# Products of ones in the gaps of `l1_attn`, a rolling order in `l1_slots`, one joined stage for `l1_combine` and `l2_attn`, and a new order in `l3_xattn`

## The reference

```python
# L1_attn: a self attention with running states; per head of 8 features, d = 8
#   states after each token = cumulative sum of outer products of k and a gradient of a layer norm,
#   applied to k (first pass) and to q (second pass), then a group norm and an output product
# L1_ffn: 64 experts, 6 per token, capacity 64, and one shared expert
scores = softmax(xf @ gate_w.T); idx = top_k(scores + gate_b, 6)
xb = zeros((64, 64, D)).at[se, pos].set(xf[tok], mode='drop')
h = silu(einsum('ecd,eid->eci', xb, w1)) * einsum('ecd,eid->eci', xb, w3)
yb = einsum('eci,edi->ecd', h, w2)
y = zeros_like(xf).at[tok].add(contrib * wf[:, None])
z = silu(xf @ ws1.T) * (xf @ ws3.T) @ ws2.T          # x + (y + z)
# L2_attn: linear attention
q, k, v = split(layernorm(x) @ W_qkv.T, 3); q = relu(q) + 1e-6; k = relu(k) + 1e-6
kv = einsum('bnd,bne->bde', k, v); z = 1 / (einsum('bnd,bd->bn', q, k.sum(1)) + 1e-6)
x + einsum('bnd,bde,bn->bne', q, kv, z) @ W_out.T + b_out
# L3_xattn: 16 heads of 8 features, 128 queries against 120 context rows, softmax, output product
```

## Time and profile before

| What | us |
|---|---|
| Median of 3 runs | 4386.08 |
| Lowest and highest run | 4382.82 and 4388.71 |
| The profiled execution, device time | 4399.44 |
| Its span, first to last instruction | 4397.5 |
| Mean granted clock | 0.817 |
| TensorE busy (share of the span) | 3267.4 (74%) |
| VectorE busy | 2842.7 (65%) |
| ScalarE busy | 1802.4 (41%) |
| GpSimd busy | 681.8 (16%) |

### The profile page before, as it was taken

One profiled execution on the slowest core, in us unless ns is written; L12 is line 12 of the kernel. 1 busy time (PEld: TensorE's weight loads), 2 busy tenths in 40 slices (PEclk: granted clock), 3 DMA queues, 4 the chain that ended last, 5 costly groups with the idle time before them and its releaser, 6 DMA issues. The chain is left out here.

```text
span 4397.5 us, 70729 instructions
## 1 busy us (share of the span) xinstructions
PE 3267.4 (74%) x22305; PEld 2394.5 (54%) x22369; DVE 2842.7 (65%) x8231; ACT 1802.4 (41%) x5188; POOL 681.8 (16%) x867
## 2 busy tenths in 40 slices
PE   3668379366654886755777876999899997786887
PEld 3546269222222664534454754666577775554777
DVE  6556633499995876174898263555467775556997
ACT  1346334111112664212777233222155553435886
POOL 0045533100002777200000120000100000000000
PEclk9789589666666665577788685999999998998999
DMA  4040168200004000420300011333200000000000
GB/s 116 1 166 0 33 195 234 73 0 0 0 0 154 3 0 1 126 95 18 74 0 0 1 38 34 103 100 99 86 1 0 0 0 4 0 0 15 1 0 19
DMA packets 135723, 196.88 MB, mean 45 GB/s; under 512 B 24858, under 2 KB 90840, under 8 KB 133846
## 3 DMA queue, kind: packets, MB, share of 16 engines
q1 hardware_dynamic: 124078, 186.31, 14.0%
q0 software_dynamic: 11520, 9.05, 0.7%
HBM read 151.49 MB, written 58.63 MB: 48 GB/s over the span
## 5 line engine op out<-in xcount | busy, mean ns | idle before, releaser
L1260 PE MATMUL l_attn_p_s<-l_attn_outer,l_attn_upper 128*128 128x512 f32 x256 | 204.5, 973 | 113.9 <-DVE l_attn_outer L1203 100.0
L95 POOL TENSOR_TENSOR rstd<-vareps,minus_half 128x32 f32<-128x32 f32 x11 | 59.9, 5444 | 1391.7 <-DVE vareps L86 1258.0
L2583 ACT ACTIVATE l_ffn_sg<-l_ffn_p_g 128x512 f32<-128x512 f32 x168 | 100.3, 597 | 355.4 <-PE l_ffn_p_g L2620 355.4
L2554 DVE TENSOR_TENSOR l_ffn_part<-l_ffn_sg,l_ffn_share 128x512 f32<-128x512 f32 x168 | 116.3, 693 | 190.8 <-ACT l_ffn_sg L2583 183.3
L2610 PEld LDWEIGHTS l_ffn_p_o<-l_ffn_wd,l_ffn_h 128*128 128x128 f32 x1344 | 175.7, 191 | 85.2 <-issue 76.1
L1418 POOL DMA_INDIRECT slots_in<-l_xattn_x,l_xattn_slot x192 | 190.3, 991 | 83.8 <-issue 49.9
L1260 PEld LDWEIGHTS l_attn_p_s<-l_attn_outer,l_attn_upper 128*128 128x128 f32 x256 | 79.2, 324 | 218.7 <-issue 174.4
L2730 ACT ACTIVATE l_attn_E<-l_attn_p_s,l_attn_nm 128x128 f32<-128x128 f32 x512 | 181.2, 386 | 2.9 <-DVE l_attn_nm L2688 2.9
L2610 PE MATMUL l_ffn_p_o<-l_ffn_wd,l_ffn_h 128*128 128x128 f32 x1344 | 178.1, 275 | 2.3 <-DVE l_ffn_h L2557 1.6
L2620 PE MATMUL l_ffn_p_g<-l_ffn_f_xTall,l_ffn_wg 128*128 (+1 forms) x336 | 173.7, 599 | 0.5 <-DVE l_ffn_turned L2545 0.5
L2622 PE MATMUL l_ffn_p_u<-l_ffn_f_xTall,l_ffn_wu 128*128 (+1 forms) x336 | 172.5, 595 | 0.0
(11 more groups left out here) (806 smaller groups left out, 9436.5 us busy)
## 6 DMA issues: line engine op xcount, KB each, us to landing
l_experts_w<-in_L_ffn_w SPq DMA_DIRECT2D x72, 512.0 KB
l_ffn_share<-share_rows SPq DMA_DIRECT2D x112, 256.0 KB, 3.2
slots_in<-l_xattn_empty SPq DMA_DIRECT2D x8, 2145.0 KB, 24.0
shares_out<-l_xattn_zero SPq DMA_DIRECT2D x24, 512.0 KB, 11.5
l_combine_got<-shares_out SPq DMA_DIRECT2D x16, 768.0 KB, 4.5
l_attn_toep<-kernel_rows SPq DMA_DIRECT2D x1, 8192.0 KB, 31.1
xattn_toep<-ssm_rows SPq DMA_DIRECT2D x1, 8192.0 KB
l_slots_w<-in_L_ffn_w SPq DMA_DIRECT2D x32, 176.0 KB
```

What stands on the lines that cost most here:

```text
L1260: mm = pe.matmul(p_s[:, r, a], upper[:], outer[:, r, a * 512:(a + 1) * 512], start=True, stop=True)
L2554: dve.tensor_tensor(part[:, w], sg[:, w], share[:, slot], ALU.mult).then_inc(s.share_used, 1)
L2583: act.activation(sg[:, k], p_g[:, k], ACT.Silu).then_inc(s.silu_ready, 1)
```

## The change

Four stages change, and one short fill is added.

1. `kept_warm` multiplies a bfloat16 tile of ones by itself, 128 x 512 per product, and nobody reads the result. In `l1_attn` TensorE makes ten of them ahead of the second running state, four ahead of the transposes of the context, and four ahead of the means of squares. They go into `p_t` and `p_c`, which are overwritten later by the transposes.
2. `l1_slots`: all programs are written out in steps (transposes at lag 0, hidden products at lag 1, down products at lag 2), and inputs have four buffers instead of two.
3. `l1_combine` and `l2_attn` become one stage `l1_out` of 16 pairs and lags 0 to 4, written out. Three of the six results are added on GpSimd and three on TensorE, as products with the identity into the bank of the down product. The norm is made per pair, with the power of two columns on GpSimd and the normalisation on ScalarE; the bias is added on GpSimd.
4. `l3_xattn`: L2952 and L2956 move behind L2961, and the output product goes to columns 256 to 384 of `p_c` instead of `p_r`; on VectorE the copy of the keys comes ahead of the addition to `x`, and the statistics come last.

The diff, cut to its core:

```diff
+def kept_warm(R, pe, bank, n):
+    for _ in range(n):
+        pe.matmul(bank, R.onesb[:], R.onesb[:].unsqueeze(1).broadcast_to((P, 4, P)), start=True, stop=True)
 # l1_attn, tensor
                     for b, u in item(2):
+                        for c, _ in item(1):
+                            pe.wait_ge(s.xT_ready, c + 1)
+                        kept_warm(R, pe, p_t[:], 10)
...
                     for b, u in item(3):
+                        kept_warm(R, pe, p_c[:], 4)
                         pe.wait_ge(s.ctx_ready, b + 1)
...
                     for b, u in item(2):
+                        for c, _ in item(0):
+                            kept_warm(R, pe, p_t[:], 4)
                         pe.wait_ge(s.squares_ready, b + 1)
 # l1_slots, tensor
-                with pe.Fori(0, NP // W) as i:
-                    for u in range(W):
-                        pe.wait_ge(x_in[u], (i + 1) * DMA)
-                        pe.transpose(p_x[:, u, 0:P], x[:, u, 0:D], R.ident[:]).then_inc(s.xT_psum, 1)
...
+                for item in written_out(2, NP, V):
+                    for n, u in item(0):
+                        pe.wait_ge(x_in[u], (n // V + 1) * DMA)
+                        after(pe, s.xT_ready, n - 1)
+                        pe.transpose(p_x[:, n % 2, 0:P], x[:, u, 0:D], R.ident[:]).then_inc(s.xT_psum, 1)
+                    for n, u in item(1):
+                        pe.wait_ge(s.xT_ready, n + 1)
+                        pe.wait_ge(up_in[u], (n // V + 1) * DMA)
+                        after(pe, s.h_ready, n - 1)
...
+                    for n, u in item(2):
+                        pe.wait_ge(s.h_ready, n + 1)
 # l1_out, sync
+                for tile, name in ((wg, "L1_ffn_ws1"), (wu, "L1_ffn_ws3"), (wd, "L1_ffn_ws2")):
+                    sp.dma_start(tile[:], A[name][0:1].rearrange("a p n -> p (a n)")).then_inc(s.w_in, DMA)
+                load(sp, A, s.w_in, [(wqkv, "L2_attn_W_qkv"), (wout, "L2_attn_W_out"), (bout, "L2_attn_b_out")])
 # l1_out, tensor
+                pe.wait_ge(s.w_in, 6 * DMA)
+                for item in written_out(4, PAIRS):
...
+                    for b, u in item(1):
+                        after(pe, s.x_added, b)
+                        pe.wait_ge(got_in[u], (b // V + 1) * DMA)
+                        for n in range(SPLIT, K):
+                            pe.matmul(p_d[:, 0:W], R.ident[:], got[:, u, :, n], start=(n == SPLIT), stop=False, skip_group_check=True)
+                        pe.wait_ge(s.h_ready, b + 1)
+                        for r in range(2):
+                            for f in range(FC):
+                                mm = pe.matmul(p_d[:, r * P:(r + 1) * P], h[:, u % 2, f, r * P:(r + 1) * P], wd[:, f * P:(f + 1) * P],
+                                               start=False, stop=(f == FC - 1), skip_group_check=True)
+                        mm.then_inc(s.down_psum, 1)
...
 # l1_out, gpsimd
+                    for b, u in item(2):
+                        pool.wait_ge(s.xhat_ready, b + 1)
+                        pool.tensor_tensor(pair(R.x, b), pair(R.x, b), both(bout), ALU.add).then_inc(s.xb_ready, 1)
+                    for b, u in item(0):
+                        pool.wait_ge(got_in[u], (b // V + 1) * DMA)
+                        for n in range(SPLIT):
+                            add = pool.tensor_tensor(pair(R.x, b), pair(R.x, b), got[:, u, :, n], ALU.add)
...
+                    for b, u in item(1):
+                        pool.wait_ge(s.var_ready, b + 1)
+                        pool.tensor_tensor(rs[:, u % 2], ve[:, u % 2], R.minus_half[:, 0:2], ALU.pow).then_inc(s.rstd_ready, 1)
 # l3_xattn, tensor
-                    for b, u in item(4):
-                        pe.matmul(p_r[:, 0], headsT[:], wo[:], start=True, stop=True).then_inc(s.out_psum, 1)
                     for b, u in item(2):
                         pe.wait_ge(s.shift_spread, b + 1)
-                    for b, u in item(1):
-                        pe.matmul(p_c[:, 0:SC], wkv[:, 0:P], cT[:, u % 2], start=True, stop=True).then_inc(s.kT_psum, 1)
-                    for b, u in item(2):
...
                         mm.then_inc(s.shifted_psum, 1)
+                    for b, u in item(4):
+                        pe.matmul(p_c[:, 256:384], headsT[:], wo[:], start=True, stop=True).then_inc(s.out_psum, 1)
+                    for b, u in item(1):
+                        pe.matmul(p_c[:, 0:SC], wkv[:, 0:P], cT[:, u % 2], start=True, stop=True).then_inc(s.kT_psum, 1)
                     for b, u in item(3):
                         pe.wait_ge(s.oT_ready, b + 1)
-                        after(pe, s.out_taken, b)
+                        after(pe, s.heads_ready, b)
```

More of the change, by code:

```diff
@@ L1788, in _ @@
             def _(sp):
-                with sp.Fori(0, NP // W) as i:
-                    for u in range(W):
[L1791 to L1800, removed]
+                for n in range(NP):
+                    after(sp, s.xT_psum, n + 1 - V)
+                    after(sp, s.meta_ready, n + 1 - V)
+                    sp.dma_start(x[:, n % V], xs[n]).then_inc(x_in[n % V], DMA)
+                    after(sp, s.hid_psum, n + 1 - V)
+                    sp.dma_start(w13[:, n % V], A["L1_ffn_w13"][n]).then_inc(up_in[n % V], DMA)
+                    after(sp, s.y_psum, n + 1 - V)
+                    sp.dma_start(w2[:, n % V], A["L1_ffn_w2"][n]).then_inc(down_in[n % V], DMA)
             @block.gpsimd
@@ L1813, in _ @@
             def _(act):
[L1814 to L1825, removed]
-                        after(act, R.stored[(n - 1) % V], (n - 1) // V * DMA)
-                        act.activation(y[:, (n - 1) % V], p_y[:, u, 0:P], ACT.Copy, scale=part[:, (n - 1) % V]).then_inc(s.y_ready, 1)
+                for item in written_out(2, NP, V):
+                    for n, u in item(1):
+                        act.wait_ge(s.hid_psum, n + 1)
+                        act.activation(sg[:, n % 2], p_h[0:FP, n % 2, 0:P], ACT.Silu).then_inc(s.silu_ready, 1)
+                    for n, u in item(0):
+                        act.wait_ge(s.xT_psum, n + 1)
+                        after(act, s.hid_psum, n - 1)
+                        act.activation(xT[:, n % 2], p_x[:, n % 2, 0:P], ACT.Copy).then_inc(s.xT_ready, 1)
+                    for n, u in item(2):
+                        act.wait_ge(s.y_psum, n + 1)
+                        act.wait_ge(s.meta_ready, n + 1)
+                        after(act, R.stored[u], n // V * DMA)
+                        act.activation(y[:, u], p_y[:, n % 2, 0:P], ACT.Copy, scale=part[:, u]).then_inc(s.y_ready, 1)
@@ L2035 @@
-PHASES.append(l2_attn)
 LAYOUTS.append(lambda a: {"L2_attn_W_qkv": transposed(a, "L2_attn_W_qkv"), "L2_attn_W_out": transposed(a, "L2_attn_W_out"),
@@ L2885, in _ @@
                                           ALU.mult).then_inc(s.heads_ready, 1)
+                    for b, u in item(4):
+                        if isinstance(b, int):
+                            dve.wait_ge(s.out_taken, b + 1)
+                        chain(dve.bn_stats(R.bn[:, u], row(R.x, b)))
+                        chain(dve.bn_aggr(R.aggr[:, u], R.bn[:, u]))
+                        if u == PER - 1:
+                            dve.tensor_copy(R.stats[:, bass.ds(b - (PER - 1), PER), :], R.aggr[:, 0:PER])
             @block.scalar
@@ L3232, in decoder @@
         R.ones = sb("ones", [P, P])
+        R.onesb = sb("onesb", [P, P], BF16)
         R.ctxT = sb("ctxT", [DC + 1, NB, SC])
```

342 lines of the change are left out of this document (171 added, 171 removed).

## The result

The changed kernel takes **4256.89 us** (median of 4 runs, 4253.62 to 4261.88) against 4387.4 us for the kernel before on the same chip (4 runs): a ratio of 0.9704, 95% interval 0.9687 to 0.9721, or 130.5 us less. Predicted were 4268 us, 118 us less, in a range of 4236 to 4312. The profiled execution took 4255.3 us (span 4253.5), against 4399.4 us of the one before.

A forecast was written before the change was run, and what follows sets the result against it. Bounds were read per stretch: VectorE in `l1_attn`, TensorE in `l1_slots` and `l3_xattn`, engines taking turns in `l1_combine` and `l2_attn`. Terms -17 - 4 - 78 - 19 = -118 us gave 4268 us on the median, range 4236 to 4312.

The forecast's parts named there:

- Ones, -17: In `l1_attn`, products of ones make the first running state fast in most periods: 80% of VectorE's 20.7 us of waits go.
- the lower price: In `l1_attn`, a 512-column product of ones costs 0.41 us at half clock, half a float32 record; the upper bound was 0.88.
- a fast second state lengthens the gap ahead of the context to some 5 us: In `l1_attn`, a second state at full clock ends 3 us earlier; the following 2.3 us gap grows, four products filling 0.9.
- clock above 0.85: Sign to look for afterwards: the clock of `l1_attn` is above 0.85; it averaged 0.66 before.
- Rival (b): In `l1_attn`, the ones don't hold the clock for the first state; 17 us go, giving 4285 us; chance 17%.
- Slots, -4: In `l1_slots`, the new order hides TensorE's idle 4.5 us of 77.5; -4 us, from -8 to +5.
- Rival (c): `l1_slots` reaches full clock once its gaps are closed: 32 us more gained, 4236 us; chance 7%.
- Joined stage, -78: `l1_combine` and `l2_attn` joined: TensorE bounds steps of 7.8 us, the stage takes 142 us against 219.8.
- Rival (a): The joined stage goes by its chain, not by TensorE: 10 us a step gives 4296 us, 11 gives 4309; chance 17%.
- `l3_xattn`, -19: In layer 3's cross attention, two products moved beside the exponential save 0.63 us in about 30 periods; between -12 and -20.
- L2952 and L2956 stand in it from 3810.04 to 3810.67, 0.63 us: In `l3_xattn`, these two products lie in the period's chain of scores, maximum, transposed scores, shift and exponential, costing 0.63 us.
- Rival (d), late instructions: Written-out steps on TensorE and SP wait for instructions, 4.5 us each: +243 us, 4511 us; chance 2%.

The follow-up runs named there:

- ones_ten: Changed kernel keeping only the ten products of ones ahead of the second running state, both groups of four removed: 4266.4 us in one execution, `l1_attn` 536.3 us.
- out_chain: Changed kernel with two more unread powers of two columns on GpSimd ahead of the real one in each `l1_out` step: steps 7.44 us, stage 10.6 us longer.
- slots_first: Changed kernel with two bfloat16 products of ones behind each pair's transpose in `l1_slots`, for the first 8 of 32 pairs only: stage 78.7 us, against 82.3.
- x3_switch: Changed kernel with one 16-column bfloat16 product between the two groups of 32-row products in `l3_xattn`: stage 282.9 us (+10.3), one execution.

## Why the prediction was right

The time lies in the range, and in each of the four stages the wait or idle time that was named is what went. Two sizes were off to the good side by some 9 and 6 us, and `l1_attn` fell 2 us short; one step of the working for `l1_attn` did not happen.

- **Ones, -17, measured -14.7.** The waits fell to 5.1 us as forecast, and a product of ones took 0.23 us at full clock and 0.445 at half (4.45 us for ten), so the lower price was the right one, and at full clock half of it. The Trainium skill ("TensorE: Matmul & The Clock Gate", Back-to-back issue gap) has 0.43 at half clock; the measured 0.445 agrees. Missing was the wait behind: the output product gave 2.3 us back. The remark that a fast second state lengthens the gap ahead of the context to some 5 us is right for `ones_ten` (5.06), but it is not what the changed kernel does. The ten were priced at half clock, where they fill two thirds of the gap; at full clock they fill 2.3 of 6.5 us, and the second state takes 5.1 to 6.6 us in every period. The first state takes 3.70 us in about half of the periods and some 5.3 in the others, and VectorE waits for a state only four times in all. So the size of the gain came out though the second state never was fast, which is luck in that step. The sign "clock above 0.85" was narrowly missed (0.84) and is a poor one: 0.74 came with no gain at all. Rival (b) is what `ones_ten` shows, and not what the change does.
- **Slots, -4, measured -4.6.** TensorE was busy for 66.89 of 70 us in the middle of the stage before (1778 to 1848 us) and for 62.56 of 63 after (from 1752 us on), 96% and 99%, at 0.50. Rival (c) supposed that closed gaps raise the clock; they don't.
- **Joined stage, -78, measured -87.3.** TensorE bounds it and the chain has the 1 us of slack. By terms: start 5.3 us (5 predicted), steps 0 to 2 14.9 (17; the fourth gate product starts at 1850.59), thirteen steps 93.1 (101), last steps 16.3 (16), clearing 2.8 (3). The mis-sized term is the step, 7.16 instead of 7.8. The ten changes of group, 0.14 us in the prediction, cost nothing. The rows for small products were taken too high: eight records of 128 columns take 0.89 us here (1905.74 - 1904.85) and not 1.05, probably since the rows of `l2_attn` still held short waits for other engines; the memory takes 0.81 instead of 0.90, two transposes 0.25 instead of 0.35, which was half of a value at half clock. Rival (a) needed a chain longer than the step; `out_chain` shows what it would have looked like. That a TensorE without idle time holds the full clock came true in these steps, but `l1_slots`, 99% busy at 0.50, shows that the absence of idle time is no ground to forecast it from.
- **`l3_xattn`, -19, measured -25.2.** The step that failed is "L2952 and L2956 stand in it from 3810.04 to 3810.67, 0.63 us". It took the two products' own time for the whole of what they cost. What a full product between groups of 32-row products costs is its time and 0.11 us at each change: 0.84 us a period times 30 is 25.
- **Rival (d), late instructions:** nothing of it is seen; from 1851 to 1943.7 us every step of the joined stage is new code, and TensorE has no idle time.

## What to carry to other kernels

Products that keep the clock up pay only in front of a product that somebody waits for; follow the gap that they open elsewhere, and judge by the waits, not by the mean clock. Where stages are joined so that one engine never idles, price its step from rows in which it does not idle, and give the first and last steps the whole chain. Keep products of one tile form together, and in a queue put the step that others wait for ahead of the sums that have time.

## What the runs showed of the hardware

- A TensorE that is 99% busy can stay at 1.2 GHz: `l1_slots` had 62.56 busy of 63 us at 0.50, with products of 64 and 128 columns; two bfloat16 products of 512 columns a pair brought 1.00 within three pairs. Once up, the clock stayed at 1.00 over 16 us of the small products alone (`slots_first`). The Trainium skill ("TensorE: Matmul & The Clock Gate", What's actually happening) lets the clock follow how busy the engine has been; by busy time alone, as the profile counts it, the row at 0.50 speaks against it.
- Small float32 products don't quite halve with the doubled clock: a record of 64 columns takes 0.159 us at half clock and 0.088 at full, start to start.
- A change between products of 32 rows and full ones costs 0.11 us (`x3_switch`).
- The same code of `l1_xattn` took 401.2 to 409.6 us from one execution to the next; why stays open.
